# One-hot matrices from spread rows of target numbers on ScalarE, and scores spread by bf16 products, in a graph layer

## What is computed

```
def _forward(x, edge_index, ...):
    proj = (x @ gat_w.T).reshape(n, NH, FOUT)
    s_src, s_tgt = sum(proj * gat_a_src), sum(proj * gat_a_tgt)
    e = leaky_relu(s_src[src] + s_tgt[tgt], 0.2)
    exp_e = exp(e - max(e))
    denom = segment_sum(exp_e, tgt)
    agg = segment_sum(proj[src] * (exp_e / (denom[tgt] + 1e-16))[:, :, None], tgt)
    h_local = layer_norm(elu(agg + x + gat_b))
    perm = argsort(degree + deg_noise)
    y = mamba(x[perm])          # a scan over the 6250 nodes: h = dA * h + dBx, y = h @ C
    h_attn = layer_norm(x + y[inv])
    gate = sigmoid(h_local @ wl.T + h_attn @ wg.T)
    h = gate * h_local + (1 - gate) * h_attn
    return layer_norm(h + feed_forward(h))
x = x + _forward(layernorm(x), [src, dst], ...)
x = x + experts(layernorm(x))   # 8 experts, two per node
```

## Time and profile before

| | us |
|---|---|
| median of 3 runs | 4477.08 (4472.79 to 4479.05) |
| the profiled execution: its own time | 4468.9 |
| its span, first to last instruction | 4467.2 |
| `both_loops`, roughly 812 to 3500 of the span | 2690 |
| stretch 900 to 3300, read below as the steady loop | 2400 |

### The profile page before, as it was taken

One profiled execution on the slowest core, in us unless ns is written; L12 is line 12 of the kernel. 1 busy time (PEld: TensorE's weight loads), 2 busy tenths in 40 slices (PEclk: granted clock), 3 DMA queues, 4 the chain that ended last, 5 costly groups with the idle time before them and its releaser, 6 DMA issues. The chain is left out here.

```text
span 4467.2 us, 66228 instructions
## 1 busy us (share of the span) xinstructions
PE 3254.4 (73%) x18333; PEld 2554.5 (57%) x18334; DVE 3342.3 (75%) x6618; ACT 1430.2 (32%) x2818; POOL 2574.3 (58%) x2215
## 2 busy tenths in 40 slices
PE   5344220488878878888888888888888488848998
PEld 4333210366666666666666666666666345527887
DVE  5677793699988988899888898989888568831111
ACT  2000000244433344333443333443333256622222
POOL 2000004477777777777777777777777246643443
PEclk8555555599999999999999999999999699979999
DMA  3000201233333333333333333333335523326665
GB/s 109 20 0 0 96 1 59 75 97 97 97 96 98 99 96 96 95 95 98 97 96 96 96 97 98 96 97 96 93 99 91 109 58 98 85 84 151 143 143 110
DMA packets 217329, 397.02 MB, mean 89 GB/s; under 512 B 49239, under 2 KB 137544, under 8 KB 216776
## 3 DMA queue, kind: packets, MB, share of 16 engines
q0 software_dynamic: 119472, 287.74, 26.3%
q1 hardware_dynamic: 97560, 105.54, 7.7%
HBM read 330.21 MB, written 62.91 MB: 88 GB/s over the span
## 5 line engine op out<-in xcount | busy, mean ns | idle before, releaser
L664 POOL DMA_INDIRECT el_g<-table,el_ix x1792 | 2026.4, 1131 | 623.2 <-issue 455.3
L1050 PE MATMUL fl_ps<-el_g,el_oh 128*128 128x260 f32 x3584 | 935.3, 406 | 303.3 <-DVE ACC L773 300.3
L1050 PEld LDWEIGHTS fl_ps<-el_g,el_oh 128*128 128x128 f32 x3584 | 695.0, 200 | 662.1 <-issue 534.2
L929 ACT COPY el_oht<-fl_pt 128x512 f32<-128x512 f32 x452 | 262.7, 581 | 1217.3 <-PE fl_pt L1027 1217.3
L793 DVE TENSOR_TENSOR_SCAN mb_h<-mb_dA,mb_h,mb_dB 128x224 f32<-128x224 f32 x896 | 572.9, 669 | 85.3 <-issue 62.4
L763 DVE TENSOR_TENSOR el_g<-el_g 128x1024 f32<-128x1024 f32 x448 | 544.3, 1215 | 0.0
L1039 PEld LDWEIGHTS fl_px<-tile_score,el_oht 128*128 128x128 f32 x3608 | 484.1, 198 | 72.4 <-issue 53.5
L1039 PE MATMUL fl_px<-tile_score,el_oht 128*128 x3608 | 456.0, 256 | 28.3 <-issue 27.3
L1073 PE MATMUL fl_py<-mb_hc,ident 128*128 128x448 f32 x896 | 436.6, 570 | 0.1
L938 ACT ACTIVATE mb_dA<-mb_dt,mb_a 128x224 f32<-128x224 f32 x898 | 382.9, 476 | 106.4 <-DVE mb_dt L854 104.6
L1027 PE MATMUL fl_pt<-ident,el_oh 128*128 128x128 f32 x1808 | 302.4, 292 | 151.2 <-DVE el_oh L730 150.4
(11 more groups left out here) (290 smaller groups left out, 5161.4 us busy)
## 6 DMA issues: line engine op xcount, KB each, us to landing
el_g<-table,el_ix POOLq DMA_INDIRECT x1792, 2.8
ex_w<-in_moe_W SPq DMA_DIRECT2D x56, 512.0 KB
ex_x<-routed_x SPq DMA_DIRECT2D x56, 257.0 KB, 2.7
mb_x<-sorted_x SPq DMA_DIRECT2D x30, 224.0 KB, 2.8
table<-px_tr POOLq DMA_DIRECT2D x49, 130.0 KB, 2.4
px_x<-in_x SPq DMA_DIRECT2D x49, 128.0 KB, 2.8
xn<-XN SPq DMA_DIRECT2D x1, 6272.0 KB
sorted_y<-mb_or SPq DMA_DIRECT2D x28, 224.0 KB, 2.5
```

The lines of the kernel that those rows point to most:

```text
L664: pool.indirect_dma_start(out=G[b // GU][:, b % GU * NJ + j, :], out_offset=None, in_=dram["table"], in_offset=bass.IndirectOffsetOnAxis(a ...
L1050: mm = nc.tensor.matmul(pS[:], OH[:, n % (2 * GU), j, :], G[n // GU % 2][:, n % GU * NJ + j, :], start=j == 0, stop=j == NJ - 1)
```

## The change

The one-hot matrix is now made on the other side. `pair_tables` writes the relative target numbers as rows in bf16 to a DRAM table `dst_rows` and no longer transposes them. In the loop SP loads one row of 512 numbers a slot and spreads it over all 128 partitions (`el_dst`, 4 buffers). ACT makes |number - partition| (`el_away`) and then relu(1 - that), which is the turned one-hot matrix `el_oht` in bf16. PE spreads the scores from it at once: the 8 numbers of a node are cut into three bf16 parts each, whose sum is the float32 number, and the mask is one more, so 25 columns. PE's `turn` now goes the other way, from `el_oht` to the matrix `el_oh` that the sums need, in bf16, and ACT copies it out as float32. DVE's `hot` is gone; DVE adds the three parts with a `tensor_reduce` once in four slots, one more instruction in `logits`; and the copy of the last state (L804 before) is ACT's `keep_last`. The diff, cut to its core:

```diff
+        srcT, parts = sb("eg_src", [P, QT * P, NJ], I32), sb("eg_parts", [P, NT, SPREAD], BF16)
...
@@ -529,26 +535,29 @@
+            done(nc.vector.tensor_copy(parts[:, :, 0:2 * NH], TSC[:]))
+            done(nc.vector.tensor_tensor(REST[:], TSC[:], parts[:, :, 0:2 * NH], ALU.subtract))
+            done(nc.vector.tensor_copy(parts[:, :, 2 * NH:4 * NH], REST[:]))
+            done(nc.vector.tensor_tensor(REST[:], REST[:], parts[:, :, 2 * NH:4 * NH], ALU.subtract))
+            done(nc.vector.tensor_copy(parts[:, :, 4 * NH:6 * NH], REST[:]))
+            done(nc.vector.memset(parts[:, :, 6 * NH:], BIG))
+            done(nc.vector.tensor_scalar(parts[:, NT - 1, 6 * NH:], w["part"][:], float(LAST), BIG, ALU.is_lt, ALU.mult))
             for t in range(QT):
                 dve.wait_ge(gathered, 2 * 16 * (QT))
                 done(nc.vector.tensor_copy(GF[:, 0, t, :], GI[:, 0, t, :]), wait=False)
                 done(nc.vector.tensor_copy(GF[:, 1, t, :], GI[:, 1, t, :]))
-                done(nc.vector.tensor_scalar(GF[:, 1, t, :], GF[:, 1, t, :], KC[:, t:t + 1], None, ALU.add))
+                nc.vector.tensor_scalar(DR_[:, t, :], GF[:, 1, t, :], KC[:, t:t + 1], None, ALU.add).then_inc(rowed, 1)
             nc.vector.tensor_copy(TH[:, 1:2], TH[:, 0:1]).then_inc(copied, 1)
             for t in range(QT):
-                for s_, dst in ((0, srcT), (1, dstT)):
...
-                    m = 2 * t + s_
-                    dve.wait_ge(turned, 1 + 2 + m)
-                    nc.vector.tensor_copy(dst[:, t * P:(t + 1) * P, :].rearrange("p q j -> p j q"),
-                                          pT[m % 4][:]).then_inc(copied, 1)
+                dve.wait_ge(turned, 1 + 2 + t)
+                nc.vector.tensor_copy(srcT[:, t * P:(t + 1) * P, :].rearrange("p q j -> p j q"), pT[t % 4][:]
+                                      ).then_inc(copied, 1)
...
             pe.wait_ge(copied, 1 + 1)
-            for m in range(2 * QT):
-                if m >= 4:
-                    pe.wait_ge(copied, 1 + m - 2)
+            for t in range(QT):
                 for j in range(NJ):
-                    mm = nc.tensor.transpose(pT[m % 4][:, j, :], GF[:, m % 2, m // 2, j * P:(j + 1) * P], w["ident"][:])
+                    mm = nc.tensor.transpose(pT[t % 4][:, j, :], GF[:, 0, t, j * P:(j + 1) * P], w["ident"][:])
...
@@ -621,7 +631,9 @@
         dA, dB, H, HC = (sb(f"mb_{n}", [P, 2, KD, TC]) for n in ("dA", "dB", "h", "hc"))
         H0 = sb("mb_h0", [P, KD, NS])
         Y, O, OR = sb("mb_y", [P, KD, TC]), sb("mb_o", [P, KD, TC]), sb("mb_or", [RB, TS, D])
-        pT, pX, pS = ps("fl_pt", [P, NJ, P]), ps("fl_px", [P, GU * NJ, 3 * NH]), ps("fl_ps", [P, ROW])
+        pT = ctx.enter_context(nc.psum_tensor("fl_pt", [P, 2 * NJ, P], BF16))[:, 0:NJ, :]
+        pX, pS = ps("fl_px", [P, 512]), ps("fl_ps", [P, 512])[:, 0:ROW]
+        pX = pX[:, 0:GU * NJ * SPREAD].rearrange("p (c s) -> p c s", s=SPREAD)
         pBC = [ps(f"fl_pbc{b}", [P, 2, TC]) for b in range(2)]
...
+            def rows(p):
+                if not early(p.number, 4):
+                    sp.wait_ge(s["away"], p.number - 3)
+                sp.dma_start(DST[:, p.n % 4, :], dram["dst_rows"][bass.ds(p.number, 1), :].rearrange("o e -> (o e)"
+                             ).partition_broadcast(P)).then_inc(brought[p.n % 4], 16)
             def slot(S):
                 c, at = S.of(NS), S.n % NS
+                rows(S + 4)
                 if at == 2:
                     load(c + 2)
                 if at == 6 and not early(c, 1):
                     store(c - 1)
+            for u in range(4):
+                rows(Slot(0, u))
             load(0)
             load(1)
             run(sp, slot)
...
-            dve.wait_ge(s["set"], 6)
-            def hot(p):
-                q, n = p.number, p.n
-                if not early(q, 2 * GU):
-                    dve.wait_ge(s["summed"], q - 2 * GU + 1)
-                nc.vector.tensor_tensor(
-                    OH[:, n % (2 * GU)], w["iota"][:, 0:P].unsqueeze(1).to_broadcast([P, NJ, P]),
-                    dstT[:, bass.ds(q, 1), :].rearrange("p o j -> p (o j)").unsqueeze(2).to_broadcast([P, NJ, P]),
-                    ALU.is_equal).then_inc(s["hot"], 1)
+            dve.wait_ge(s["set"], 8)
...
-                nc.vector.tensor_tensor(Z[:], G[g][:, :, D:], pX[:, :, 0:NH], ALU.add).then_inc(s["logit"], 1)
+                nc.vector.tensor_reduce(S8[:], pX[:, :, 0:6 * NH].rearrange("p c (s v) -> p c v s", v=2 * NH), AX_X, ALU.add
+                                        ).then_inc(s["logit"], 1)
                 yield
-                dve.wait_ge(s["logit"], grp * 4 + 1)
+                dve.wait_ge(s["logit"], grp * 5 + 1)
+                nc.vector.tensor_tensor(Z[:], G[g][:, :, D:], S8[:, :, 0:NH], ALU.add).then_inc(s["logit"], 1)
+                yield
+                dve.wait_ge(s["logit"], grp * 5 + 2)
                 nc.vector.scalar_tensor_tensor(L[:], Z[:], 0.2, Z[:], ALU.mult, ALU.max).then_inc(s["logit"], 1)
                 yield
-                dve.wait_ge(s["logit"], grp * 4 + 2)
-                nc.vector.tensor_tensor(DM[:], L[:], pX[:, :, NH:2 * NH], ALU.subtract).then_inc(s["logit"], 1)
-                nc.vector.scalar_tensor_tensor(Q[:], pX[:, :, 2 * NH:], -BIG, L[:], ALU.add, ALU.add
-                                               ).then_inc(s["logit"], 1)
+                dve.wait_ge(s["logit"], grp * 5 + 3)
+                nc.vector.tensor_tensor(DM[:], L[:], S8[:, :, NH:], ALU.subtract).then_inc(s["logit"], 1)
+                nc.vector.scalar_tensor_tensor(Q[:], pX[:, :, 6 * NH:].to_broadcast([P, GU * NJ, NH]), -BIG, L[:], ALU.add,
+                                               ALU.add).then_inc(s["logit"], 1)
                 yield
-                dve.wait_ge(s["logit"], grp * 4 + 4)
+                dve.wait_ge(s["logit"], grp * 5 + 5)
...
@@ -801,7 +819,6 @@
                     dve.wait_ge(s["y"], m - 1)
                 nc.vector.tensor_tensor(HC[:, n % 2], H[:, n % 2], pBC[n % 2][:, 1, :].unsqueeze(1).to_broadcast([P, KD, TC]),
                                         ALU.mult).then_inc(s["hc"], 1)
-                nc.vector.tensor_copy(H0[:, :, n % NS], H[:, n % 2, :, TC - 1]).then_inc(s["h0"], 1)
...
-                if not last:
-                    hot(S + GU)
                 if not early(S.number, 1):
                     read_out(S - 1)
-                parts = logits(S) if n % GU == 0 and not last else None
-                if parts:
-                    next(parts)
...
-            for u in range(GU):
-                hot(Slot(0, u))
...
@@ -919,14 +933,35 @@
         def _(act):
             act.wait_ge(s["weights"], 144)
             nc.scalar.activation(AE[:], A[:], ACT.Exp).then_inc(s["rate"], 1)
+            act.wait_ge(s["set"], 8)
+            def one_hot(p):
+                q, n = p.number, p.n
+                act.wait_ge(brought[n % 4], p.of(4) * 16 + 16)
+                if not early(q, 1):
+                    act.wait_ge(s["hot"], q)
+                nc.scalar.activation(AWAY[:], DST[:, n % 4, :], ACT.Abs, bias=LESS[:, 0:1]).then_inc(s["away"], 1)
+                if not early(q, 2):
+                    act.wait_ge(s["turned"], q - 1)
+                    act.wait_ge(s["spread"], q - 1)
+                act.wait_ge(s["away"], q + 1)
+                nc.scalar.activation(OHT[:, n % 2, :], AWAY[:], ACT.Relu, bias=1.0, scale=-1.0).then_inc(s["hot"], 1)
             def keep_turned(p):
                 q, n = p.number, p.n
                 act.wait_ge(s["turned"], q + 1)
-                if not early(q, 2):
-                    act.wait_ge(s["spread"], q - 1)
-                nc.scalar.copy(OHT[:, n % 2], pT[:]).then_inc(s["turned_sb"], 1)
+                if not early(q, 2 * GU):
+                    act.wait_ge(s["summed"], q - 2 * GU + 1)
+                nc.scalar.copy(OH[:, n % (2 * GU)], pT).then_inc(s["turned_sb"], 1)
+            def keep_last(p):
+                m, n = p.number, p.n
+                act.wait_ge(s["h"], (m + 1) * KD)
+                nc.scalar.copy(H0[:, :, n % NS], H[:, n % 2, :, TC - 1]).then_inc(s["h0"], 1)
...
-                keep_turned(S + GU)
+                if not early(S.number, 1):
+                    keep_last(S - 1)
+                one_hot(S + GU)
+                keep_turned(S + (GU - 1))
...
-            for u in range(GU):
-                keep_turned(Slot(0, u))
+            one_hot(Slot(0, 0))
+            for u in range(1, GU):
+                one_hot(Slot(0, u))
+                keep_turned(Slot(0, u - 1))
...
-                    mm = nc.tensor.transpose(pT[:, j, :], OH[:, n % (2 * GU), j, :], w["ident"][:])
+                    mm = nc.tensor.transpose(pT[:, j, :], OHT[:, n % 2, j * P:(j + 1) * P], I16[:])
...
-                pe.wait_ge(s["turned_sb"], q + 1)
+                pe.wait_ge(s["hot"], q + 1)
...
-                    mm = nc.tensor.matmul(pX[:, n % GU * NJ + j, :], OHT[:, n % 2, j, :],
```

(6 more changed lines are left out.)

66 lines of the change are left out of this document (38 added, 28 removed).

## The result

The changed kernel takes 4502.38 us (median of 4 runs, 4499.13 to 4507.28), the kernel before 4478.07 in the same comparison (4472.79 to 4479.94): ratio 1.0059, 95% interval 1.0043 to 1.0075. It is **slower by 24 us**; 46 were forecast. The profiled execution spans 4497.8 us, against 4467.2.

A forecast was written before the change was run, and what follows sets the result against it. GpSimd (POOL), full to 98%, was taken as the bound: gathers 5.00 + index copy 0.06 + holding loss 0.91 = 5.97 us a slot against 5.87, 46 us more over 448 slots, so 4515 profiled, median 4523, range 4500 to 4560.

The forecast's parts named there:

- walk of a plain slot: Gathers against VectorE's order after the change: two held, losing 0.42 and 0.78, 1.20 us together; two run free.
- POOL is where the end is set: GpSimd, full to 98% with the same four gathers, sets the loop's time; only less loss per gather could gain.
- The wait behind the chunk load: Row load queued behind the chunk load: ACT waits 2 to 3 us once a chunk, covered; uncovered 56 us.
- Near 0.58: ACT's new operations on 128x512 were each to take about 0.58 us.
- The reduction: DVE's added reduction over 384 numbers from PSUM, once in four slots: 0.54 us, or 0.13 a slot.
- DVE below 80%: Sign that the forecast is right: VectorE busy under 80%.
- Its longest total wait at the reduction: Sign of being right: DVE waits over 400 us there, for the group's last gather or PE's spread behind it.
- The clock within 0.05 of 0.96: Sign of being right: PE's mean granted clock stays within 0.05 of 0.96.
- rival C: TensorE's clock falls as PE waits longer, 4613 us; or the chunk load's wait is uncovered, 4579; chance 0.17.
- POOL idle beyond its gaps: Sign of being wrong: over 5%, meaning PE at 1.2 GHz or ACT waiting at the row loads bounds instead.
- B: VectorE was the bound: the slot falls by 0.62 us, 278 us less, 4199; chance 0.01.
- A: Gathers' hold points fall evenly: loss 0.65 a slot, slot 5.71, 72 us less, 4405; chance 0.25.

The follow-up runs named there:

- one edit on one chain: Changed kernel with eight row buffers, rows asked eight tiles ahead: 1.0018 of the kernel before; changed kernel with scale in four pieces instead: 1.0068.
- an edit on each of two chains: Changed kernel with eight row buffers and scale cut into four pieces of 128x256: 4472.19 us, 0.9973 of the kernel before.

## Why the forecast was right, and where it was not

**Sign and size.** The steady tile was put at 5.97 and is 5.97; the tile before at 5.87 and is 5.88. From the first to the last gather the changed kernel takes 36.6 us more (2704.1 against 2667.5), where 46 were forecast; the loop begins 3.8 us earlier (setup put at 0, within 4), and 2.3 us come off behind it. Together that is the 30.6 us between the spans. Between the medians it is 24.3, about half of what was forecast: the profiled execution lies 9 us under its median before and only 3 us after, where the forecast carried the 8 over.

**The gathers.** Mean 1163 ns, inside 1.16 to 1.19. In the walk of a plain slot two gathers were to lose 0.42 and 0.78, so to take 1.37 and 1.73. A plain slot in the trace:

```profile
1538.99 1.26 POOL L676 DMA_INDIRECT el_g<-table,el_ix  x1 [0.30 <-issue]
1540.56 1.29 POOL L676 DMA_INDIRECT el_g<-table,el_ix  x1 [0.30 <-issue]
1542.15 1.78 POOL L676 DMA_INDIRECT el_g<-table,el_ix  x1 [0.31 <-issue]
1544.24 0.94 POOL L676 DMA_INDIRECT el_g<-table,el_ix  x1 [0.30 <-issue]
```

Here three gathers lose time, 0.32, 0.35 and 0.84 us, 1.5 together for the 1.20 of the walk. Over the stretch the pair of 1.37 and 1.73 didn't come: gathers of 1.32 to 1.42 us fell from 121 to 16, and those of 1.68 to 1.85 rose from 100 to 260. The direction of the walk is right all the same. Take for each gather the VectorE instruction in progress 0.13 us after its start, and sum what the gather took beyond 0.945: `scale` cost 185.6 us before (381 gathers, 0.49 each) and costs 255.7 after (396, 0.65 each), the scans 81.8 and 78.6, and `hot` had cost only 18.3. Gathers run into `scale` earlier than before: that adds 45 ns to the mean gather, and `hot` gone takes 11 off.

The Trainium skill's lock ("SBUF — State Buffer", section "SBUF: two separate sides") agrees with the third of them: `scale` runs from 1541.90 to 1543.12, and the third gather, issued into it, ends 0.81 after it. The section would let one expect only relief from removing `hot`; the gathers got 34 ns longer, as the forecast had it.

**The step that failed is "POOL is where the end is set".** POOL is full, 4 x (1.163 + 0.30) + 0.02 for its copy = 5.87 of 5.97, and still not the one that decides alone: with half the gathers the kernel gains 28 us, 0.6%, or 0.9% by the ratios to the kernel before, where GpSimd as the only bound would have given over 250 us. The forecast read fullness as being the bound. The gathers are issued into eight buffers; POOL works through DVE's long slots and through its short ones alike, and that it is full doesn't show that it is late. That another chain was at the same height, the forecast had as a rival, at 0.17, and not as company. The agreement of the sum to 0.01 us a tile is therefore partly luck: the same 5.97 comes from ACT's and PE's side. Inside the sum two errors cancel as well: the held gathers lose 0.87 us a tile for 0.91 and the index copy costs 0.02 for 0.06, while POOL's waits for PE, put at nothing without a reason, are still about 0.10 (523.1 us idle in 402 tiles, 1.30, less four gaps of 0.30).

**The wait behind the chunk load** was seen, but sized at 2 to 3 us once a chunk and taken as covered. ACT waits 221.2 us in 50 waits, two in each chunk, 8.8 us a chunk, up to 8.2 at once. The row was said to land 3.4 us after PE's transposes; it does so some 4.5 after them (1542.59 to 1547.06). The larger mistake is when ACT wants it: it stands there from 1547.06 - 7.73 = 1539.33 on, 3.3 us before PE has turned the chunk, where the forecast had it arrive as the row lands. ACT runs further ahead of PE than the forecast allowed. And it isn't covered: DVE's wait at slot 4 is this wait, 5.96 us in the chunk shown. Removing it gained what separates 1.0059 from 1.0018 and no more, because the gathers then end the same wait (121.8 us in slot 4).

**Sizes of ACT.** "Near 0.58" was 0.721 for the absolute value and 0.630 for the relu; the row load lands in 3.3 us on the median, not 2.8. ACT's work still rose only from 2.32 to 3.63 us a tile (3.67 forecast), since instructions overlap in the timeline: L950 ends at 1548.44, and the copy behind it starts at 1548.35. **PE**: spread and turn come to 4 x (0.176 + 0.229) = 1.6 us as summed durations, but they overlap; by busy time (103.7 + 166.4) / 402 they are 0.67, against 1.65 before, under the 0.8 taken, which was also the lower bound. PE is busy 4.40, not 4.0: its sums take 984.4 / 402 = 2.45 us a tile, against 1.99 for a tile at the upper clock in the earlier trace rows. **The reduction**: 0.557 for 0.54.

**What was to be seen.** DVE below 80%: 79%. Its longest total wait at the reduction: yes, but 272 us, not over 400. The clock within 0.05 of 0.96: wrong, 0.87; this part of rival C did come. The clock also fell when only `hot` was left out of the kernel before (0.92), and in the chunk shown it fell in the course of six microseconds with 1.68 us of PE's work: it goes along with PE's waits. What the lower clock costs in time wasn't tried. POOL idle beyond its gaps: 101.9 us at most, 4%, under the 5% set. That bar could not have shown the error, as the run with half the gathers proves. **VectorE's work**: 4.74 a tile, not 4.52. Mean durations overstate what goes: DVE's instructions overlap by some 0.08 us, and leaving out `hot`, 0.682, took 0.60 off its work in the run that did only that. With L804 at about 0.12 and the reduction at about 0.12 that makes 0.60; 0.54 were measured, and 0.06 stays unexplained.

**Rivals.** B (VectorE the bound, 4199) is out: 0.6 us less of work in the kernel before costs 0.3%. A (even spread, 4405) is out by the time and by the mean of 1163 ns, where it needed under 1090. C is half right: its uncovered wait and its lower clock are there, but they lie beside the gathers' lateness and not on top of it, and the price is within the forecast's sum instead of 50 to 90 us above it.

## What to carry over

When three engines are at 78 to 90% and each waits a little for the others, account for the engine that all of them meet: its work plus its waiting per tile, and who ends the waits. Work taken off it comes back as waiting unless every chain that ends at the same wait is shortened; here, among the kernels that keep the result, one edit on one chain was worth 0.4% at best, and an edit on each of two chains 0.9%. Leaving out half of one chain's work outright was worth no more than that. An engine whose queue is full is not thereby the bound; halve its work in a kernel that gives up the result, and see. And before loads are put into a queue with a blocking wait in it, ask when the engine behind them wants the first one held up, not only when it is issued.

## What the runs showed of the hardware that was not expected

- A full GpSimd queue that isn't the bound: half of the indirect gathers removed, 4502 to 4474 us; the gathers left take 1108 ns.
- ACT's absolute value and relu on 128x512 in bf16 take 721 and 630 ns, more than its copy from PSUM of the same shape in fp32, 581.
- GpSimd's copy of 128x64 integers, 724 ns in the earlier trace rows, takes 247 ns in the changed kernel: in the timeline 1546.43, 0.25 us, beside a DVE that waits. It was held by VectorE: of 25 copies in the steady stretch before, 20 began inside `scale` and ended 0.09 us behind it (785 to 810 ns), 3 did the same behind `hot` (562 to 567), and 2 met neither (252). With `hot` left out none is held (248).
- A gather is also held by a DVE instruction with one fp32 input in SBUF (L857 of the changed kernel, 0.38 us): two that were issued just after its start took 1.13 and 1.14 us and ended 0.82 behind it.
- Two comparisons in which the kernel before took 4733 and 4738 us instead of 4480, with engines waiting 2 to 9 us for releases long past; with half of the gathers it took 4496. The traces don't show what stalls there.
